# Degrees of an attention graph by way of DRAM, and its two layers on two head pairs at once

## The chip, the cores and the metric

One core of one Trainium2 chip runs the whole program. The metric is device time in microseconds (us); three runs of the kernel before gave 1188.17, 1189.1 and 1192.54 us.

## What is computed

The input has 16 batches of 256 tokens of 128 numbers. Each batch goes through an attention with 16 heads of 64 numbers, and its attention matrix also serves as a graph:

```
q, k, v = layer_norm(x) @ Wq, Wk, Wv          # 16 heads
attn = softmax(causal(q @ k.T))                # 256 x 256 per head
out  = attn @ v
adj  = clip(attn + eye, 0, 1);  deg = sum(adj, -1)
feats = v
for l in range(2):
    feats = gelu((adj @ (feats @ gnn_w[l] + gnn_b[l])) / deg + feats)
out  = layer_norm((out + feats @ lin_w + lin_b) @ Wo)
```

A mixture of 8 experts (two per token) follows; it runs as a separate stage after the 16 batches, and the change doesn't touch it, but for the loading of its weights.

The kernel does not compute attn @ v. It computes M = (adj / deg) @ v, subtracts v, and multiplies by deg: attn @ v = deg * (M - v). deg is thus wanted in a layout with the head's 64 numbers along the partitions and the 256 tokens along the free axis, the same deg in all 64 partitions of a head.

## The kernel before, in words

Heads go in 8 pairs, a pair being 128 partitions wide. Every engine has an order written out by hand in a function `batch(b, before, routed, after)`, which runs batch b and, woven in, the end of batch b-1, the routing of b-2 and the start of b+1. It is unrolled for batches 0, 1 and 15; a loop runs 2 to 14. Engines meet only through semaphores; each executes in order, so a wait holds up all that stands behind it.

The steps of pair n that matter here:

- `queries_keys`, `scores` on TensorE, `maxima` on VectorE (L1396), `exps` on ScalarE (L1118), `adjacency` on VectorE (L1406 to L1411, which also gives `den` and 1/sum in `rs`), `weights` on VectorE (L1420), `graph` on GpSimd (L495, L497: divides by the degree), `transposes` on TensorE (L743 to L746) and `graph` on ScalarE (copies into `gt0`, `gt1`).
- Degrees: GpSimd's `degrees` (L506) writes den * rs 64 times side by side into `deg`, 128x256; TensorE's `degrees` (L769) turns it with two transposes into the upper half of PSUM bank 5.
- Mixed values: TensorE's `differences` puts M into the lower half of bank 5 (8 matmul instructions); VectorE's `difference` (L1425) subtracts v into `dT`, `attended` (L1430) multiplies by the degrees in bank 5 into `aT`; ScalarE's `mixed_values` copies M into `gvT`.
- Layer 1: `layer1` on TensorE, `layer1_out` on VectorE (L1445), `gelu1` on ScalarE (L1142). Layer 2: `layer2_in` on TensorE and its copy on ScalarE, `layer2` on TensorE (8 matmul instructions), `layer2_out` on VectorE (L1451), `gelu2` on ScalarE (L1156).
- `output_attended` and `output_graph` add the pair's share of the projection in bank 7.

An f32 product shows as two matmul instructions in the trace, so one `layer1` is 2, one `layer2_in` 4. L633 is the line of the helper that issues all products. `norm_step(after, i)` and `norm_tokens(before, i)` on VectorE are the layer norms of the next and the last batch; some wait for a power taken on GpSimd (L489, L513). The queue of SyncE (SP) loads the inputs, clears `slots` in DRAM (33 DMAs of 520 KB, L364), loads the experts' weights (L373, L377: the DMA of expert e waits until expert e-2's were split by VectorE, L1458, and GpSimd, L537), and is then idle until the experts' stage. In the first batch, VectorE waits (in `small_weights` and for `w_x`) until the rest of x has landed.

Of the kernel before, what the change touches and what calls it, by code (L numbers as in the profile page):

```python
# [19 lines left out]
P = 128  # L20
BATCHES, TOKENS, DIM = 16, 256, 128
HEADS, DHEAD = 16, 64
PAIRS = HEADS // 2
TILES = TOKENS // P
# [20 lines left out]
CLEAR = 8  # L45
# [27 lines left out]
def build_program(nc, x, wq, wk, wv, wvT, gnn_w, gnn_b, lin_wT, lin_b, wo, gamma_in, gamma_out,  # L73
                  norm_w, routerT, guT, downT, alpha, slots, pairs, out):
# [9 lines left out]
    with ctx:  # L84
# [39 lines left out]
        zero = sb("zero", [P, CLEAR * ROW])  # L124
# [35 lines left out]
        gu_lo = sb("gu_lo", [P, EXPERTS, 2 * HID], f32r)  # L160

# [18 lines left out]
        deg = at("deg", [P, 3, 4, DHEAD])  # L180
# [4 lines left out]
        gvT = at("gvT", [P, PAIRS, TOKENS])  # L185
        vT = at("vT", [P, PAIRS, TOKENS])
        aT = at("aT", [P, PAIRS, TOKENS])
        f1T = at("f1T", [P, 4, TOKENS])
        g1 = at("g1", [P, 2, TILES, P])
        dT = at("dT", [P, TOKENS])  # L190
        z1 = at("z1", [P, 2, TOKENS])
        z2 = at("z2", [P, 2, TOKENS])
        f2T = at("f2T", [P, 4, TOKENS])
# [63 lines left out]
        p_deg = Signal(sem("p_deg"), PAIRS)  # L257
# [3 lines left out]
        a_d = Signal(sem("a_d"), PAIRS)  # L261
        d_d = Signal(sem("d_d"), PAIRS)
        s_deg = Signal(sem("s_deg"), PAIRS)
        d_a = Signal(sem("d_a"), PAIRS)

        s_f1, d_z1 = Signal(sem("s_f1"), PAIRS), Signal(sem("d_z1"), PAIRS)
        a_f1 = Signal(sem("a_f1"), PAIRS)
        s_g1, a_g1 = Signal(sem("s_g1"), PAIRS), Signal(sem("a_g1"), PAIRS)
        s_h2, d_z2 = Signal(sem("s_h2"), PAIRS), Signal(sem("d_z2"), PAIRS)
        a_f2, s_og = Signal(sem("a_f2"), PAIRS), Signal(sem("s_og"), PAIRS)  # L270
# [46 lines left out]
        L1_BANK, L2_IN_BANK, L2_BANK = 0, 2, 1  # L317
        MIX, DEG = slice(0, TOKENS), slice(TOKENS, 2 * TOKENS)
# [17 lines left out]
        def _(sp):  # L336
# [24 lines left out]

            sp.wait_ge(k_consts, 1)
            for r in range(0, SLOT_ROWS, CLEAR * P):
                sp.dma_start(slots[r:r + CLEAR * P, :].rearrange("(p r) d -> p (r d)", p=P),  # L364
                             zero[:, :]).then_inc(w_clear, 16)

# [7 lines left out]
            for e in range(EXPERTS):  # L374
                if e >= 2:
                    sp.wait_ge(k_gu_lo, e - 1)
                sp.dma_start(raw_gu[:, e % 2, :], guT[e]).then_inc(w_gu[e % 2], 16)  # L377
# [54 lines left out]
        def _(pool):  # L432
# [68 lines left out]
            def degrees(b, n):  # L501

                s = n % 3
                if n >= 3:
                    s_deg.wait(pool, b, n - 2)
                nc.gpsimd.tensor_tensor(deg[:, s], den[:, s, :].unsqueeze(2).to_broadcast([P, 4, DHEAD]),  # L506
                                        rs[:, s, :].unsqueeze(2).to_broadcast([P, 4, DHEAD]),
                                        ALU.mult).then_inc(p_deg.sem, 1)

# [30 lines left out]
            def batch(b, before, routed, after):  # L540

                graph(b, 0)
                degrees(b, 0)
                graph(b, 1)
                degrees(b, 1)
                graph(b, 2)
                graph(b, 3)
                degrees(b, 2)
                degrees(b, 3)
                graph(b, 4)  # L550
                if after is not None:
                    deviation(after, 0, 3)
                if before is not None:
                    token_power(before, 0)
                degrees(b, 4)
                if routed is not None:
                    d_pl.wait(pool, routed, 5)
                graph(b, 5)
# [3 lines left out]
                degrees(b, 5)  # L562
                graph(b, 6)
                graph(b, 7)
                degrees(b, 6)
                if after is not None:
                    deviation(after, 1, 7)
                degrees(b, 7)
                if after is None:
                    for e in range(0, 3):  # L570
                        gate_up_low(e)
# [4 lines left out]
                if after is None:  # L576
                    for e in range(3, 6):
                        gate_up_low(e)
                if before is not None:
                    token_power(before, 2)  # L580
                if after is None:
                    for e in range(6, EXPERTS):
# [1463 lines left out]
```

## Time and profile before

| what | us |
|---|---|
| median of three runs | 1189.1 |
| the profiled execution, its own time | 1183.16 |
| its span, first to last instruction | 1181.3 |
| TensorE busy in the span | 1088.6 |
| VectorE busy | 913.0 |
| ScalarE busy | 806.1 |
| GpSimd busy | 497.6 |

The profile is of one execution. "PE" is TensorE, "DVE" VectorE, "ACT" ScalarE, "POOL" GpSimd. A duration in the timeline is from an instruction's start to its end; neighbours on one engine overlap, so what an instruction takes from its engine is the distance from its start to the next one's start, called its pitch below. The mean granted clock of TensorE is 0.982 of full speed.

### The profile page before, as it was taken

The numbers are of one execution on the slowest core, as the hardware profiler recorded it, in microseconds if no ns is written. First come the engines' busy times: TensorE is split into PE (matmuls) and PEld (weight loads), VectorE is DVE, ScalarE is ACT, GpSimd is POOL, SyncE is SP. The second block draws the span as 40 slices with busy tenths as digits, with TensorE's granted clock in tenths as the row PEclk, the third lists the DMA queues.
The fourth block names the chain that finished last, engine by engine and source line by source line (L and its number), as shares of the span: only waits on it lengthen the run. The fifth ranks groups of instructions, "written<-read, shape, count | busy, mean of one in ns | idle before, by whom it ended". The sixth has DMA issues, their size and how long they took to land.

```text
span 1181.3 us, 28227 instructions
## 1 busy us (share of the span) xinstructions
PE 1088.6 (92%) x8320; PEld 863.9 (73%) x8320; DVE 913.0 (77%) x3755; ACT 806.1 (68%) x2351; POOL 497.6 (42%) x648
## 2 busy tenths in 40 slices
PE   5999999999999999999999999999999977898993
PEld 4677777777777777777777777777777756888993
DVE  5658797979797979797979797979788895566556
ACT  4678686768686868686868686868686853565662
POOL 4324253525353534343434344444444362545444
PEclk9899999999999999999999999999999998999997
DMA  6960000000000000000000000000000011222227
GB/s 201 405 231 1 2 3 9 5 6 3 8 3 8 1 10 1 10 1 10 1 10 1 10 1 10 1 10 1 10 1 9 2 55 49 60 55 63 62 62 221
DMA packets 37311, 47.41 MB, mean 40 GB/s; under 512 B 6009, under 2 KB 28539, under 8 KB 37200
## 3 DMA queue, kind: packets, MB, share of 16 engines
q1 hardware_dynamic: 32880, 37.81, 10.2%
q0 software_dynamic: 4320, 8.47, 2.1%
q14 instruction: 84, 0.69, 0.2%
q8 instruction: 27, 0.44, 0.2%
HBM read 18.14 MB, written 28.58 MB: 40 GB/s over the span
## 4 chain that ended last, share of the span: by engine, by line
PE 57%; DVE 29%; issue 8%; DMA 3%; SPq 1%; POOL 1%; ACT 1%; DVEq 0%; POOLq 0%
PE bank L633 46%; DVE eb L1411 5%; DVE nmax L1396 5%; DVE ea L1408 3%; PE bank L730 3%; DVE dT L1425 2%; PE bank L1000 2%; PE bank L769 1%; PE bank L743 1%; DVE z L1445 1%; DVE ratio L1755 1%; PE bank L746 1%; PE bank L744 1%; DMA pairs<-zout,zin 1%; DVE t L1656 1%
## 5 line engine op out<-in xcount | busy, mean ns | idle before, releaser
L495 POOL TENSOR_TENSOR ea<-ea,wgt 128x256 f32<-128x256 f32 x128 | 78.3, 612 | 400.1 <-DVE wgt L1420 400.1
L1396 DVE TENSOR_REDUCE nmax<-bank 128x1 f32<-128x128 f32 (+1 forms) x512 | 152.0, 346 | 60.5 <-PE bank L633 48.4
L1086 ACT ACTIVATE gt<-bank 128x512 f32<-128x512 f32 (+1 forms) x256 | 111.5, 491 | 66.6 <-PE bank L746 66.5
L1118 ACT ACTIVATE ea<-bank,nmax 128x128 f32<-128x128 f32 x256 | 96.0, 375 | 62.3 <-DVE nmax L1396 56.5
L633 PE MATMUL bank<-gt,g 128*64 128x256 f32 (+1 forms) x1024 | 112.8, 341 | 24.3 <-DVE z L1451 24.3
L497 POOL TENSOR_TENSOR eb<-eb,wgt 128x512 f32<-128x512 f32 x128 | 132.9, 1039 | 0.0
L1118 ACT ACTIVATE eb<-bank,nmax 128x256 f32<-128x256 f32 x256 | 123.3, 482 | 0.0
L633 PE MATMUL bank<-gt,vnat 128*64 128x256 f32 (+1 forms) x1024 | 111.5, 337 | 12.0 <-ACT gvT L1086 11.0
L633 PE MATMUL bank<-qk 64*128 64x128 f32 (+1 forms) x1024 | 119.3, 351 | 0.0
L1411 DVE SCALAR_TENSOR_TENSOR eb<-idw,ssum,eb 128x256 f32<-128x256 f32 x256 | 118.4, 500 | 0.0
L633 PEld LDWEIGHTS bank<-gt,g 128*64 128x64 f32 x1024 | 65.9, 137 | 61.1 <-issue 33.6
L523 POOL DMA_INDIRECT pairs<-zout,zin x71 | 69.7, 982 | 95.9 <-DVE zout L1942 89.6
L633 PEld LDWEIGHTS bank<-gt,vnat 128*64 128x64 f32 x1024 | 67.5, 136 | 58.2 <-issue 33.6
L1156 ACT ACTIVATE f2T<-z,gb 128x256 f32<-128x256 f32 x128 | 63.8, 515 | 62.3 <-DVE z L1451 62.3
L513 POOL TENSOR_TENSOR rs<-ve,half 128x2 f32<-128x2 f32 x48 | 33.3, 693 | 146.1 <-DVE ve L1701 96.1
L1451 DVE TENSOR_TENSOR z<-bank,f1T 128x256 f32<-128x256 f32 x128 | 54.1, 423 | 50.0 <-PE bank L633 48.9
L633 PEld LDWEIGHTS bank<-qk 64*128 64x128 f32 x1024 | 67.5, 187 | 27.1 <-issue 27.1
L1935 DVE TENSOR_TENSOR shid<-bank,ssg 128x352 f32<-128x352 f32 x71 | 37.2, 525 | 59.9 <-ACT ssg L1267 45.2
L1408 DVE SCALAR_TENSOR_TENSOR ea<-ident,ssum,ea 128x128 f32<-128x128 f32 x256 | 83.0, 362 | 0.0
L633 PE MATMUL bank<-gvT,gw 128*128 128x256 f32 x256 | 80.7, 397 | 1.2 <-DVE z L1445 0.2
L633 PE MATMUL bank<-xt_lo,w_hi 128*128 128x256 f32 x256 | 79.7, 311 | 2.2 <-DVE xt_lo L1389 2.2
L1086 ACT ACTIVATE qk<-bank 128x512 f32<-128x512 f32 x128 | 78.1, 610 | 5.1 <-PE bank L633 5.1
(231 smaller groups left out, 3207.9 us busy)
## 6 DMA issues: line engine op xcount, KB each, us to landing
slots<-zero SPq DMA_DIRECT2D x33, 520.0 KB, 15.2
zin<-slots SPq DMA_DIRECT2D x71, 65.0 KB
got<-pairs SPq DMA_DIRECT2D x8, 512.0 KB, 6.9
raw_gu<-in_guT SPq DMA_DIRECT2D x8, 352.0 KB, 2.9
out<-x_all SPq DMA_DIRECT2D x8, 256.0 KB, 2.6
pairs<-zout,zin POOLq DMA_INDIRECT x71
dn<-in_downT SPq DMA_DIRECT2D x2, 512.0 KB, 16.6
slots<-z,row_now POOLq DMA_INDIRECT x64, 2.3
```

The costliest lines, as they stand in the source:

```text
L495: nc.gpsimd.tensor_tensor(ea[:, s], ea[:, s], wgt[:, s, 0:2].unsqueeze(2).to_broadcast([P, 2, P]), ALU.mult)
L497: nc.gpsimd.tensor_tensor(eb[:, s], eb[:, s], wgt[:, s, 2:4].unsqueeze(2).to_broadcast([P, 2, 2 * P]), ALU.mult).then_inc(p_g.sem, 1)
L523: nc.gpsimd.indirect_dma_start(pairs, bass.IndirectOffsetOnAxis(ap=zin[:, j % RING, ID:ID + 1].bitcast(u32), axis=0), zout[:, j % RING, :] ...
L633: return nc_mm(o, st, mo, start=first, stop=last, **more)
L1086: return nc.scalar.activation(o, i, ACT.Copy, **more)
L1118: done = nc.scalar.activation(e[:, s, a, :], score_bank(n, a)[:, TILE_SCORES[t]], ACT.Exp, bias=nmax[:, s, i:i + 1], accum_out=ssum[:, s, ...
L1156: nc.scalar.activation(f2T[:, n % 4, :], z2[:, n % 2, :], ACT.Gelu, bias=gb[:, 1:2]).then_inc(a_f2.sem, 1)
L1396: done = V.tensor_reduce(nmax[:, n % 3, i:i + 1], score_bank(n, a)[:, TILE_SCORES[t]], X, ALU.max, negate=True)
L1408: V.scalar_tensor_tensor(ea[:, s, a, :], ident[:, :], ssum[:, s, a:a + 1], ea[:, s, a, :], ALU.mult, ALU.max, accum_out=den[:, s, a:a + 1])
L1411: done = V.scalar_tensor_tensor(eb[:, s, a, :], idw[:, :], ssum[:, s, 2 + a:3 + a], eb[:, s, a, :], ALU.mult, ALU.max, accum_out=den[:, s, ...
L1451: V.tensor_tensor(z2[:, n % 2, :], bank[L2_BANK][:, 0:TOKENS], f1T[:, n % 4, :], ALU.add).then_inc(d_z2.sem, 1)
L1935: V.tensor_tensor(shid[:, j % 2, 0:HID], bank[2 + j % 2][:, 0:HID], ssg[:, j % 2, :], ALU.mult).then_inc(d_hid.sem, 1)
```

## The change

Pairs 2d and 2d+1 form a double d (four in a batch, DOUBLES = 4). `differences`, `difference`, `attended`, `mixed_values`, `layer1`, `layer1_out`, `gelu1`, `layer2_in`, `layer2`, `layer2_out` and `gelu2` run once per double on 512 columns, each with one wait and one signal. The number of matmul instructions of a double is twice that of a pair.

GpSimd's and TensorE's `degrees` are gone. VectorE multiplies den * rs for a double (two instructions on 4 numbers per partition) into `dg`; SP writes these 1024 numbers, each by itself, to DRAM in the order of the tokens, waits until they have landed, and reads each row of 512 back into 64 partitions of `dgb`. VectorE's `attended` waits for that and takes both operands from SBUF.

```diff
+            def degrees(b, d):                       # sync
+                k = b * DOUBLES + d
+                d_dg.wait(sp, b, d + 1)
+                sp.dma_start(degs[2 * k:2 * k + 2, :].rearrange("a (j p) -> p (a j)", p=P),
+                             dg[:, d].rearrange("p a m t -> p (a m t)"),
+                             allow_slow_non_contiguous=True).then_inc(w_dg, 16)
+                sp.wait_ge(w_dg, 16 * (k + 1))
+                if k >= 2:
+                    sp.wait_ge(d_a.sem, k - 1)
+                for a in range(2):
+                    sp.dma_start(dgb[a * DHEAD:(a + 1) * DHEAD, d % 2, :],
+                                 degs[2 * k + a:2 * k + a + 1, :].to_broadcast([DHEAD, 2 * TOKENS])).then_inc(w_dgb.sem, 16)
...
+            pieces, ahead = SLOT_ROWS // (CLEAR * P), 9
             sp.wait_ge(k_consts, 1)
+            clear(0, ahead)
+            for k in range(2 * DOUBLES):
+                degrees(k // DOUBLES, k % DOUBLES)
+                clear(ahead + k * (pieces - ahead) // (2 * DOUBLES), ahead + (k + 1) * (pieces - ahead) // (2 * DOUBLES))
...
+            for e in range(2):
+                sp.dma_start(raw_gu[:, e % 2, :], guT[e]).then_inc(w_gu[e % 2], 16)
+            for b in range(2, BATCHES):
+                for d in range(DOUBLES):
+                    degrees(b, d)
+            for e in range(2, EXPERTS):
+                sp.wait_ge(k_gu_lo, e - 1)
...
+            def differences(b, d):                   # tensor
+                a_gt.wait(pe, b, 2 * d + 2)
+                if d >= 1:
+                    a_d.wait(pe, b, d)
+                for m in range(2):
+                    n = 2 * d + m
+                    mm = mixed(bank[5][:, m * TOKENS:(m + 1) * TOKENS],
+                               lambda t, a: vnat[:, t, n * P + a * DHEAD:n * P + (a + 1) * DHEAD], n)
+                mm.then_inc(s_mix.sem, 1)
...
-            def attended(b, n):                      # vector
-                d_d.wait(dve, b, n + 1)
-                V.tensor_tensor(aT[:, n, :], bank[5][:, DEG], dT[:, :], ALU.mult).then_inc(d_a.sem, 1)
+            def degrees(b, d):
+                d_e.wait(dve, b, 2 * d + 2)
+                for m in range(2):
+                    s = (2 * d + m) % 3
+                    done = V.tensor_tensor(dg[:, d, :, m, :].rearrange("p a t -> p t a"),
+                                           den[:, s, :].rearrange("p (t a) -> p t a", t=TILES),
+                                           rs[:, s, :].rearrange("p (t a) -> p t a", t=TILES), ALU.mult)
+                done.then_inc(d_dg.sem, 1)
+            def attended(b, d):
+                d_d.wait(dve, b, d + 1)
+                w_dgb.wait(dve, b, 32 * (d + 1))
+                V.tensor_tensor(aT[:, 2 * d:2 * d + 2, :], dgb[:, d % 2, :].rearrange("p (n i) -> p n i", n=2),
+                                dT[:, :].rearrange("p (n i) -> p n i", n=2), ALU.mult).then_inc(d_a.sem, 1)
```

All four orders in `batch` are written anew for the doubles. Those that the steps of the prediction speak of: in VectorE's,

```diff
                 maxima(b, 0, 1)
+                if before is None:
+                    small_weights()
+                    dve.wait_ge(w_x, 16)
...
+                maxima(b, 1, 0)
+                adjacency(b, 0)
...
-                maxima(b, 1, 1)
-                if before is None:
-                    small_weights()
-                    dve.wait_ge(w_x, 16)
...
+                weights(b, 2)
+                degrees(b, 0)
+                maxima(b, 4, 0)
+                maxima(b, 4, 1)
+                norm_step(after, 3)
+                adjacency(b, 3)
+                adjacency(b, 4)
+                weights(b, 3)
+                output_bias(before)
+                weights(b, 4)
+                norm_step(after, 4)
+                maxima(b, 5, 0)
+                maxima(b, 5, 1)
+                degrees(b, 1)
+                difference(b, 0)
+                output_kept(before)
+                adjacency(b, 5)
+                maxima(b, 6, 0)
+                weights(b, 5)
+                attended(b, 0)
...
+                layer1_out(b, 2)
+                norm_tokens(before, 6)
+                norm_tokens(before, 7)
+                degrees(b, 3)
+                norm_tokens(before, 8)
+                attended(b, 2)
+                x_low(after)
+                difference(b, 3)
```

and in TensorE's, for the end of a batch,

```diff
+                output_attended(b, 0)
+                layer1(b, 0)
+                output_attended(b, 1)
+                differences(b, 2)
+                layer1(b, 1)
+                transposes(b, 6)
+                layer2_in(b, 0)
+                layer1(b, 2)
+                layer2(b, 0)
...
+                layer2_in(b, 1)
+                output_attended(b, 2)
+                transposes(b, 7)
+                layer2(b, 1)
+                differences(b, 3)
+                layer2_in(b, 2)
+                output_graph(b, 0)
+                output_graph(b, 1)
+                layer1(b, 3)
+                layer2(b, 2)
+                output_graph(b, 2)
+                layer2_in(b, 3)
+                queries_keys(after, 0, b)
+                tokens_transposed(before, bank[6], after)
+                layer2(b, 3)
+                output_graph(b, 3)
+                queries_keys(after, 1)
+                values(after, 0, b)
```

Three of the last batch's `output_attended` more (3 to 7 instead of 5 to 7) run after it. `zero`, the source of the clears, now lies in the memory of `gu_lo`, and `gvT`, `f1T` and `f2T` hold two doubles each.

## Rows read from the trace of the kernel before

**Rows 1.** Busy by stretch, one turn, last batch: us, PE, PEld, DVE, ACT, POOL; clock, DMA.

```profile
617.50:677.10 59.60, 57.09 (x447) 43.76 (x446) 49.81 (x217) 43.81 (x135) 24.93 (x33) 1.00 0.02 5
...
915.50:975.00 59.50, 51.44 (x392) 39.47 (x390) 53.58 (x200) 39.47 (x123) 30.90 (x35) 0.97 0.10 30
```

**Rows 2.** Chain that ended last, one turn: start, us, what.

```profile
657.73 0.42 DVE z L1451
...
692.49 0.92 DVE ratio L1755
...
717.33 0.42 DVE z L1451
```

**Rows 3.** Timeline, TensorE: start, us, line, count.

```profile
607.37 0.87 PE L633 MATMUL bank<-gt,g 128*64 128x256 f32 x8
608.17 0.44 PE L769 MATMUL bank<-ident,deg 128*128 128x128 f32 x2
608.44 0.60 PE L633 MATMUL bank<-gvT,gw 128*128 128x256 f32 x2
608.88 0.61 PE L633 MATMUL bank<-gw,f1T 128*128 128x128 f32 x4
609.32 1.46 PE L633 MATMUL bank<-f2T,lwo 128*128 128x256 f32 x6
610.62 0.59 PE L633 MATMUL bank<-gvT,gw 128*128 128x256 f32 x2
```

**Rows 4.** Timeline, VectorE: start, us, line, count.

```profile
641.72 0.17 DVE L1406 RECIPROCAL rs<-ssum 128x4 f32<-128x4 f32 x1
...
643.14 0.42 DVE L1425 TENSOR_TENSOR dT<-bank,vT 128x256 f32<-128x256 f32 x1
643.47 0.17 DVE L1420 RECIPROCAL wgt<-den 128x4 f32<-128x4 f32 x1
643.60 0.42 DVE L1430 TENSOR_TENSOR aT<-bank,dT 128x256 f32<-128x256 f32 x1
...
648.89 1.14 DVE L1396 TENSOR_REDUCE nmax<-bank 128x1 f32<-128x128 f32 x4
649.95 0.41 DVE L1445 TENSOR_TENSOR z<-bank,vT 128x256 f32<-128x256 f32 x1
```

**Rows 5.** Groups of the loop by form: busy, mean ns of one.

```profile
L1396 DVE TENSOR_REDUCE nmax<-bank 128x1 f32<-128x256 f32 x176 | 72.8, 413 | 0.0
...
L1396 DVE TENSOR_REDUCE nmax<-bank 128x1 f32<-128x128 f32 x176 | 49.0, 278 | 35.1 <-PE bank L633 23.2 <-issue 11.1
```

**Rows 6.** Timeline, VectorE: three waits inside an instruction.

```profile
632.87 0.91 DVE L1755 TENSOR_SCALAR ratio<-ratio 128x2 f32<-128x2 f32 x1
...
638.82 0.52 DVE L1773 TENSOR_TENSOR place<-pre_sb,next_row 128x32 f32<-128x32 f32 x1
...
655.62 2.19 DVE L1656 TENSOR_SCALAR t<-y_now,mv,rs 128x128 f32<-128x128 f32 x2
```

**Rows 7.** Timeline, GpSimd, at the same times.

```profile
632.72 1.04 POOL L497 TENSOR_TENSOR eb<-eb,wgt 128x512 f32<-128x512 f32 x1
...
638.26 1.04 POOL L497 TENSOR_TENSOR eb<-eb,wgt 128x512 f32<-128x512 f32 x1
...
656.69 1.03 POOL L497 TENSOR_TENSOR eb<-eb,wgt 128x512 f32<-128x512 f32 x1
```

**Rows 8.** DMAs: size and median from issue to landing.

```profile
got<-pairs SPq DMA_DIRECT2D x8, 512.0 KB, 6.9
raw_gu<-in_guT SPq DMA_DIRECT2D x8, 352.0 KB, 2.9
...
gout<-in_gamma_out SPq DMA_DIRECT2D x1, 64.0 KB, 2.5
...
normw<-in_norm_w SPq DMA_DIRECT2D x1, 0.5 KB, 2.1
```

**Rows 9.** Waits in the first batch: us, times, longest.

```profile
DVE stat L1349 <- DMA x_all<-in_x: 4.8, 1, 4.8
```

More of the change, by code:

```diff
@@ L561, in batch @@
                         scatter(routed, c)
-                degrees(b, 5)
-                graph(b, 6)
                 graph(b, 7)
[L565 to L568, printed above, removed]
                 if after is None:
-                    for e in range(0, 3):
+                    for e in range(0, 2):
                         gate_up_low(e)
@@ L791, in layer2_in @@
[L791 to L805 removed]
+                    d_z1.wait(pe, b, d)
@@ new lines, in layer1, with layer2_in @@
+                for m in range(2):
+                    mm = product(bank[L1_BANK][:, m * TOKENS:(m + 1) * TOKENS], gw[:, 0, :], gvT[:, 2 * (d % 2) + m, :],
+                                 True, True)
+                mm.then_inc(s_f1.sem, 1)
+            def layer2_in(b, d):
+                a_f1.wait(pe, b, d + 1)
+                if L2_IN_BANKS[d] in (3, 4):
+                    a_gt.wait(pe, b, PAIRS)
+                if d >= 1:
+                    a_g1.wait(pe, b, d)
+                for i in range(2 * TILES):
+                    mm = product(bank[L2_IN_BANKS[d]][:, xt(i)], f1T[:, d % 2, xt(i)], gw[:, 1, :], True, True)
+                mm.then_inc(s_g1.sem, 1)
@@ L807, in output_start, with layer2 @@
+            def layer2(b, d):
+                a_g1.wait(pe, b, d + 1)
+                if L2_BANKS[d] in (3, 4):
+                    a_gt.wait(pe, b, PAIRS)
+                if d >= 1:
+                    d_z2.wait(pe, b, d)
+                for m in range(2):
+                    mm = mixed(bank[L2_BANKS[d]][:, m * TOKENS:(m + 1) * TOKENS],
+                               lambda t, a: g1[:, d % 2, m, t, a * DHEAD:(a + 1) * DHEAD], 2 * d + m)
+                mm.then_inc(s_h2.sem, 1)
             def output_start(b, before, routed):
@@ L937, in batch @@
-                if before is not None:
-                    tokens_transposed(before, bank[6], after)
-                if after is not None:
                     values(after, 0, b)
@@ L1182, in batch @@
                     folded_lin(0)
+                exps(b, 2, 1)
+                exps(b, 3, 0)
+                graph(b, 0)
                 exps(b, 3, 1)
-                graph(b, 1)
-                mixed_values(b, 0)
                 queries_keys(b, 5)
@@ L1201, in batch @@
                 graph(b, 4)
-                mixed_values(b, 3)
+                mixed_values(b, 1)
+                graph(b, 5)
                 exps(b, 7, 0)
@@ L1466, in batch @@
                 maxima(b, 0, 1)
-                if routed is not None:
-                    choose(routed, 1)
-                maxima(b, 1, 0)
-                adjacency(b, 0)
-                weights(b, 0)
-                maxima(b, 1, 1)
                 if before is None:
@@ L1477, in batch @@
                     norm_step(after, 0)
+                if routed is not None:
+                    choose(routed, 1)
+                maxima(b, 1, 0)
+                adjacency(b, 0)
+                if after is not None:
+                    norm_step(after, 1)
+                weights(b, 0)
+                maxima(b, 1, 1)
                 maxima(b, 2, 0)
@@ L1541, in batch @@
                     gate_up_high(0)
-                if after is not None:
-                    norm_step(after, 3)
-                layer1_out(b, 3)
+                    gate_up_high(1)
                 if after is None:
                     table_first(0)
-                weights(b, 7)
-                difference(b, 5)
-                if after is not None:
-                    norm_step(after, 4)
-                layer1_out(b, 4)
+                layer1_out(b, 2)
+                if before is not None:
+                    norm_tokens(before, 6)
+                    norm_tokens(before, 7)
```

532 lines of the change are left out of this document (211 added, 321 removed).

## The prediction

> **What bounds the kernel now.** I read the busy table by stretches first. One turn of the loop is 59.6 us, and in it TensorE is busy 57.09, VectorE 49.81, ScalarE 43.81 and GpSimd 24.93 [rows 1]. TensorE is idle for 2.5 us only. Then the chain of waits. It ends a stretch on VectorE with the `z` of 657.73, runs through TensorE alone until about 692, its products in a row without a gap, and from 692.49 to 717.33 through VectorE again, which is full there with maxima, adjacency and the small layer-norm steps; the pattern repeats after 717.33 - 657.73 = 59.60 us [rows 2]. So the turn has two limits that take turns: TensorE for 34 us, VectorE for 26 us, and in VectorE's part TensorE is nearly full too. A change that takes work off TensorE pays in the first part at once, and in the second only if VectorE gets shorter or TensorE's work moves there. What counts is the pitch, the distance between starts.
>
> **TensorE, removed.** The two transposes of a pair's degrees have a pitch of 608.44 - 608.17 = 0.27 us [rows 3]; where nothing waits it should be the 0.44 / 4 x 2 = 0.22 of two 128-column instructions of layer 2's input [rows 3]. I take 0.24. Eight of them are 1.9 us a turn. The number of all other products stays. What the doubles save is the hand-over between groups: a mixed product has a pitch of 0.80 [rows 3], while its four 256-column and four 128-column instructions, two side by side, would take 2 x 0.217 + 2 x 0.11 = 0.65 (0.217 is 1.30 / 6 from the output products, 0.11 as above [rows 3]). But layer 1's product and its neighbour have 0.44 each [rows 3], which leaves nothing to save. 16 groups go (32 become 16): between 0 and 16 x 0.15 = 2.4 us, and I take 0.05 each, 0.8 us, because most groups look like the tight ones. TensorE: -2.7 us a turn.
>
> **VectorE.** The four kinds of operation that become double took a pitch of 0.33 on 256 columns [rows 4]. Going from 128 to 256 columns adds 413 - 278 = 135 ns [rows 5], so 256 more add 0.27, and a double takes 0.60. Each kind goes from 8 x 0.33 = 2.64 to 4 x 0.60 = 2.40; four kinds save 1.0 us. The eight small products den * rs are new, at the 0.13 of a small operation in the queue (643.60 - 643.47, the pitch of `weights` [rows 4]): 1.0 us. VectorE comes out even, so its 26 us don't shrink by its own work.
>
> **ScalarE and GpSimd.** ScalarE's fixed cost is paid 16 times less; it is not on the chain, so this is worth nothing beyond the slack it gives. GpSimd loses eight `degrees`, some 5 of its 24.93 us, and is on the chain only through holds of VectorE (below).
>
> **What of it lies on the path.** Walking through the new orders with these pitches, TensorE's own work is some 54 to 55 us a turn. I find three places where it waits. `layer1` of double 1 wants bank 0 back from `layer1_out` of double 0, which stands in VectorE's order behind the placing of tokens: about 1.3 us. `layer1` of double 2 wants the same and `mixed_values`: about 1 us. And `transposes` of pair 7 wants GpSimd, which has the four scatters in front of its last `graph`: some 0.6 us. That is 2.9 us against the 2.5 us idle of now, the same within what such a walk can tell. I therefore take the turn to be shorter by TensorE's saving: -2.7 us.
>
> **The new wait.** `attended` now waits for two DMAs in series: the write of 1024 single numbers, and the read of rows into 64 partitions. No row shows such a write. A DMA of 128 single numbers lands in 2.1 us [rows 8]; if more pieces cost nothing this is the lower end. The upper end is by the 512 pieces of 1 KB of `got`, 6.9 us: (6.9 - 2.1) / 384 = 12.5 ns a piece makes 13.3 us for 1024. Those move 512 KB each and run several at a time, ours 4 KB and alone, so I take 4.2 us, nearer to the low end. The read is like the load of `gout`, one row spread over partitions, 2.5 us [rows 8]. With 0.8 for SP's two hand-overs and the second read's issue (an estimate), the chain takes 7.5 us, with ends 5.1 and 16.6.
>
> The Trainium skill's page "DMA: Bandwidth & Descriptors" says in its rules for kernel authors that a non-contiguous last dimension becomes one descriptor per element, and in its specifications that pieces below 512 B are read, modified and written. It names no time for a 4-byte write, and speaks for the upper half of the range.
>
> How much stands between `degrees` and `attended` on VectorE? For double 0: five maxima at 0.53 (1.06 / 2 [rows 4]), three `adjacency` at 1.42 (643.14 - 641.72 [rows 4]), three `weights`, the small `norm_step` and output steps (some 1.7 in all), two small products and one `difference`: about 9.8 us. Double 1 has about 11, double 2 about 9, by the same count. Double 3 has only 5.5 of work, but in TensorE's part VectorE also waits, and nothing needs it before the next batch's scores, some 4 us later. So 7.5 us is covered everywhere, 9 us just so. Behind a late `attended` stand `maxima`, and so `exps` and all the rest of the batch.
>
> **Once only.** In the first batch VectorE's wait for the rest of x (4.8 us [rows 9]) moves ahead of two maxima, one `adjacency` and one `weights`: 2 x 0.53 + 1.42 + 0.13 = 2.6 us of work is now done after it, which eats that batch's 2.7. In the last batch the load of expert 2's weights stands on SP behind the last degrees: 4.2 + 0.3 for the write, some 0.8 of issues, 2.9 for the load [rows 8], less about 2.7 of VectorE's work in between, gives a stall of 5.5 us before its split; against -2.7 that is +3. The clears, spread over two batches instead of one, are needed by batch 2 only; nothing waits for them, and a degree's write finds at most three of them in front of it and mostly none. Moving `zero` and the smaller buffers costs nothing: a buffer of two doubles holds the same four pairs as before, and `gvT`'s smaller room is behind a product that is long done.
>
> **Sum.** Fourteen turns (batches 1 to 14) at -2.7 are -38; the first batch 0, the last +3: -35 us. From the profiled execution's 1183.16 us that is 1148 us; its time lies 5.9 below the median of 1189.1, so against the median it is 1154.
>
> **Rival 1, the degrees come late (slower).** The place is `attended` of doubles 0 and 2; a stall at 0 gives double 1 its room, one at 2 gives it to 3. With a chain of L us a turn pays (L - 9.8) + (L - 9). At 10.75 this is 2.7 and the gain is gone; at 12 it is 5.2, so +2.5 a turn, +35 in all, 1224 us; at the upper end of 16.6 it is over 1340. For it: 1024 separate writes, and nothing in the profile that has the like. Against it: every small DMA here lands in 2.1 to 2.9 us.
>
> **Rival 2, GpSimd holds VectorE.** A `ratio` step on two numbers took 0.91 us, from 632.87 to 633.78, while GpSimd worked from 632.72 to 633.76; two layer-norm steps together took 2.19 us until 657.81, GpSimd until 657.72; a product of 32 columns with both operands in SBUF took 0.52 [rows 6, 7]. `attended` read its degrees from PSUM until now and reads both operands from SBUF in the new kernel; the eight small products do too. Twelve such instructions, GpSimd busy for a third of the turn (20 of 59.6), half a GpSimd operation of 1.04 each time: 12 x 1/3 x 0.5 = 2 us, of which some 1.3 would fall where VectorE is the limit. The turn then gains 1.4 and the time is 1189.1 - 20 + 3 = 1172. Against it: GpSimd has 5 us less to do, so that the old holds (1.65 us in the layer-norm steps alone) become rarer. The Trainium skill's "GPSIMD Engine Reference", key points, has the same rule: GpSimd shares its SBUF interfaces with VectorE, which contend for instructions in a two-port mode or with two SBUF inputs. By that rule, the rows agree.
>
> **Rival 3, coarser steps.** Each link of the layers' chain (product, add, gelu, product, copy, product) is longer by 0.27 and more, and only four doubles are there to overlap instead of eight pairs. If TensorE's waits in its own part grow by the 2.7 that it saves, nothing is won: 1189 to 1192. For it: the three waits found above are all of this kind. Against it: the new orders put other work (projection, next batch's queries) between the links.
>
> **How the numbers follow.** The forecast (the degrees covered, TensorE's saving comes through, with 2 to 4 us a turn) has 0.52; rival 2 has 0.18, rival 3 0.12, rival 1 0.18. The likeliest time is 1154. The low end takes the whole 2.4 of hand-overs and a fifth fewer holds: -4.3 a turn, -60, +3, so 1132; the high end takes in rivals 2 and 3 and the mildest of rival 1: 1200. A measurement of this kernel can tell about 0.5% (6 us) from no change. Faster: the forecast and rival 2 and a sliver of the third, 0.72. Same: 0.08. Slower: rival 1 and the rest of 3, 0.20.
>
> **What would show it.** In the changed kernel's trace: a turn of about 56.9 us; no line of degrees' transposes; TensorE's idle time in a turn still about 2.5; SP's write landing in about 4 us and the read in 2.5; no idle time of VectorE in front of `attended`. An `attended` of well over 0.6 us, ending with an operation of GpSimd, would be rival 2; idle time in front of it until a DMA, rival 1; TensorE idle until `z` or `gvT`, rival 3. A turn of 59 us or more makes the prediction wrong.

## The result and the profile after

The changed kernel takes 1400.9 us (median of four, 1394.4 to 1406.9), the kernel before 1188.6 beside it: a ratio of 1.178 [1.172, 1.184]. Times below are medians of the fast executions; one of e7's four, 1258.1 us, was over 1.5% above the fastest and is left out. The forecast was 1154 and its range ended at 1200, so it was wrong in sign and far outside. What came is Rival 1's mechanism, at more than Rival 1's price. The page of the profile after, its busy times, chain and costliest waiting group (the two profiled executions took 1406.93 and, before, 1183.16 us):

```profile
PE 1124.7 (80%) x8064; PEld 880.6 (63%) x8064; DVE 846.2 (60%) x3627; ACT 768.5 (55%) x2095; POOL 426.9 (30%) x520
...
DMA 40%; PE 29%; issue 13%; DVE 11%; SPq 5%; ACT 1%; POOL 0%; DVEq 0%; POOLq 0%
...
L1425 DVE TENSOR_TENSOR aT<-dgb,dT 128x512 f32<-128x512 f32 x64 | 45.1, 704 | 253.8 <-DMA dgb<-degs 253.7
```

A 40% share of DMA in the chain says that engines stand still for transfers, and the last line says where: 253.7 us in front of `attended`. Its own 704 ns are what it takes without any transfer too (708 in a turn of e1, below), so it isn't Rival 2. The turn from 720.09, measured between two copies of `pre_sb`, is 71.94 us instead of 59.60 [rows 1], with no more work in it but a lower clock:

```profile
720.09:792.03 71.94, 57.62 (x430) 43.25 (x430) 45.36 (x211) 41.74 (x119) 20.46 (x25) 0.93 0.11 19
```

SyncE's timeline (start and duration are of the issues) and VectorE's degrees and `attended` in the same time:

```profile
704.74 0.36 SPq L370 DMA_DIRECT2D degs<-dg  x1
715.03 1.08 SPq L377 DMA_DIRECT2D dgb<-degs  x2
716.16 0.59 SPq L370 DMA_DIRECT2D degs<-dg  x1
725.43 1.08 SPq L377 DMA_DIRECT2D dgb<-degs  x2
729.82 0.36 SPq L370 DMA_DIRECT2D degs<-dg  x1
739.64 1.35 SPq L377 DMA_DIRECT2D dgb<-degs  x2
741.03 0.59 SPq L370 DMA_DIRECT2D degs<-dg  x1
```

```profile
711.78 0.67 DVE L1407 TENSOR_TENSOR dg<-den,rs 128x4 f32<-128x4 f32 x2
718.54 0.69 DVE L1425 TENSOR_TENSOR aT<-dgb,dT 128x512 f32<-128x512 f32 x1 [3.13 <-DMA dgb<-degs]
728.95 0.69 DVE L1425 TENSOR_TENSOR aT<-dgb,dT 128x512 f32<-128x512 f32 x1 [3.63 <-DMA dgb<-degs]
729.56 0.23 DVE L1407 TENSOR_TENSOR dg<-den,rs 128x4 f32<-128x4 f32 x2
748.03 0.69 DVE L1425 TENSOR_TENSOR aT<-dgb,dT 128x512 f32<-128x512 f32 x1 [8.52 <-DMA dgb<-degs]
```

Three things can be read off. From the issue of the write to that of the read, which waits for it, 715.03 - 704.74 = 10.3 us pass, then 9.3 and 9.8: not the 4.2 of the forecast. The degrees of double 1 are ready at about 712, but SP takes them at 716.16 only, because until then it stood at double 0's write. And the read issued at 739.64, with the slow write of double 3 right behind it, lands at 748.0, after 8 us. The write itself is not moving data all that time (stretches of the changed kernel; the last two columns are the DMA engines' share and GB/s):

```profile
705.00:706.00 1.00, 1.00 (x9) 0.95 (x8) 1.00 (x6) 0.77 (x4) 1.00 (x2) 1.00 0.25 2
706.00:707.00 1.00, 1.00 (x7) 0.91 (x6) 1.00 (x7) 1.00 (x7) 0.28 (x1) 1.00 0.21 2
707.00:708.00 1.00, 1.00 (x6) 0.62 (x4) 1.00 (x8) 1.00 (x4) 0.00 (x0) 1.00 0.00 0
```

Its pieces pass from 705 to 707, and the share is 0.00 from there to 715, until its landing is signalled. The Trainium skill's page "DMA: Bandwidth & Descriptors", in "Anatomy of one DMA", puts most of a transfer's fixed time, which it gives as about 2.0 us and constant, on the receipt of the write from memory, HBM being the heaviest. It speaks there of transfers issued by GpSimd; this one is SP's. The eight silent microseconds agree with the place, and not with the figure.

Cut into parts by the first and the last of the 14 copies of `pre_sb` up to the last batch's and by the first load of the experts' stage, in us:

| | first batch until | a turn, mean of 13 | last part |
|---|---|---|---|
| before | 162.0 | 59.58 | 46.7 |
| changed | 221.6 | 71.24 | 60.2 |
| without the transfers (e1) | 162.2 | 56.12 | 43.6 |
| slow writes that nobody waits for (e7) | 180.0 | 60.88 | 62.3 |

### The profile page after: what moved, and what is told of

Its sections match the earlier page's. It is cut to its first block, busy times and chain, and to the rows that moved or that the text cites. A ratio compares the mean times of both kernels' runs of the same rounds, so it can differ in the third digit from the quotient of the medians.

```text
span 1405.1 us, 27144 instructions
## 1 busy us (share of the span) xinstructions
PE 1124.7 (80%) x8064; PEld 880.6 (63%) x8064; DVE 846.2 (60%) x3627; ACT 768.5 (55%) x2095; POOL 426.9 (30%) x520
## 4 chain that ended last, share of the span: by engine, by line
DMA 40%; PE 29%; issue 13%; DVE 11%; SPq 5%; ACT 1%; POOL 0%; DVEq 0%; POOLq 0%
DMA degs<-dg 29%; PE bank L639 25%; DMA dgb<-degs 10%; SPq L377 3%; DVE nmax L1376 2%; DVE eb L1392 2%; PE bank L992 2%; DVE ea L1389 1%; DMA x_all<-in_x 1%; PE bank L974 1%; DMA raw_gu<-in_guT 1%; PE bank L740 1%; SPq L364 1%; DVE x_all L1967 0%; DVE dg L1407 0%
## 5 line engine op out<-in xcount | busy, mean ns | idle before, releaser
L1425 DVE TENSOR_TENSOR aT<-dgb,dT 128x512 f32<-128x512 f32 x64 | 45.1, 704 | 253.8 <-DMA dgb<-degs 253.7
L639 PE MATMUL bank<-gvT,gw 128*128 128x256 f32 x256 | 89.5, 483 | 110.7 <-ACT gvT L1080 73.9
L639 PEld LDWEIGHTS bank<-gvT,gw 128*128 128x128 f32 x256 | 56.9, 239 | 129.4 <-ACT gvT L1080 114.5
L1080 ACT ACTIVATE gvT<-bank 128x512 f32<-128x512 f32 x64 | 38.5, 602 | 166.4 <-DVE dT L1417 151.2
L639 PE MATMUL bank<-gt,g 128*64 128x256 f32 (+1 forms) x1024 | 118.3, 382 | 8.8 <-ACT g L1080 8.4
L639 PE MATMUL bank<-gt,vnat 128*64 128x256 f32 (+1 forms) x1024 | 100.6, 340 | 15.4 <-ACT gt L1080 14.6
L639 PEld LDWEIGHTS bank<-gt,g 128*64 128x64 f32 x1024 | 74.5, 159 | 56.8 <-issue 28.8
L639 PE MATMUL bank<-xt_lo,w_hi 128*128 128x256 f32 x256 | 89.1, 348 | 1.6 <-DVE xt_lo L1369 1.6
L639 PE MATMUL bank<-gw,f1T 128*128 128x128 f32 x512 | 74.4, 291 | 19.3 <-ACT f1T L1139 18.2
L1153 ACT ACTIVATE f2T<-z,gb 128x512 f32<-128x512 f32 x64 | 46.2, 722 | 74.1 <-DVE z L1449 74.1
```

Source lines behind the costliest of these rows:

```text
L639: return nc_mm(o, st, mo, start=first, stop=last, **more)
L1080: return nc.scalar.activation(o, i, ACT.Copy, **more)
L1153: nc.scalar.activation(f2T[:, d % 2, :], z2[:, d % 2, :], ACT.Gelu, bias=gb[:, 1:2]).then_inc(a_f2.sem, 1)
L1425: V.tensor_tensor(aT[:, 2 * d:2 * d + 2, :], dgb[:, d % 2, :].rearrange("p (n i) -> p n i", n=2), dT[:, :].rearrange("p (n i) -> p n i", n ...
```

## The experiments

Theory A: it is the length of the chain write, read, `attended`, and what makes the write long is that its pieces are neighbours in memory. Theory B: making 1024 pieces costs it. Later a third stood beside them: the slow writes also hold up transfers with which they have nothing to do.

**m1, what a small transfer costs.** The kernel before, with 40 small DMAs on SP in a time when its queue is free, each waited for before the next.

```diff
+                for r in range(4):
+                    probe(tr_a[2 * r:2 * r + 2, :].rearrange("a (j p) -> p (a j)", p=P), pr[:, 0:8], ...)
...
+                    probe(tr_d[r, :, 0:1].rearrange("(j p) o -> p (j o)", p=P), pr[:, 0:8], ...)
```

> The kernel before, with 40 small DMAs on SP after the loads of the weights of experts 0 and 1, each waited for before the next is issued; nothing reads what they move. Theory A (the memory's confirmation of many 4-byte writes to DRAM is what takes the time; their packets moved in 2 us and then nothing moved for 8 us): 1024 numbers of 4 bytes to DRAM in the changed kernel's order land in 9 to 10 us; 128 pieces of 32 bytes in 2 to 2.5 us; 256 pieces of 16 bytes in 2.5 to 4 us; 256 single numbers in about 4 us; 1024 numbers with 64 bytes between them also in about 9 us if the count matters, in 3 to 4 us if neighbours in one line of memory hold each other up; 1024 single numbers read from DRAM in 3 to 4 us. Theory B (making the descriptors takes the time, whichever side they are on): the gather of 1024 single numbers from DRAM takes 9 to 10 us as well, and so do the spaced ones. Both: a row of 512 numbers spread over 64 partitions lands in 2.5 to 3 us; the kernel's own time stays at 1189 us.

SyncE's timeline of m1, a row for each kind, with its count:

```profile
75.91 31.39 SPq L370 DMA_DIRECT2D tr_a<-gu_lo  x4
115.26 5.45 SPq L370 DMA_DIRECT2D tr_b<-gu_lo  x4
121.80 23.62 SPq L370 DMA_DIRECT2D tr_c<-gu_lo  x4
153.33 9.33 SPq L370 DMA_DIRECT2D tr_d<-gu_lo  x4
165.07 6.31 SPq L370 DMA_DIRECT2D tr_a<-gu_lo  x4
173.57 13.93 SPq L370 DMA_DIRECT2D gu_lo<-gu_lo  x8
188.90 20.48 SPq L370 DMA_DIRECT2D gu_lo<-tr_a  x8
211.70 7.29 SPq L370 DMA_DIRECT2D gu_lo<-tr_b  x4
```

One takes the distance to the next row by the count. 1024 numbers side by side, as in the changed kernel: (115.26 - 75.91) / 4 = 9.8 us. 128 pieces of 32 B: 1.6. 256 single numbers side by side: 7.9. 1024 single numbers 64 B apart: (165.07 - 153.33) / 4 = 2.9. 256 pieces of 16 B: 2.1. The read of one row into 64 partitions: (211.70 - 188.90) / 8 = 2.85. The last row is 1024 single numbers read from DRAM; from its first issue to its fourth it is (7.29 - 0.36) / 3 = 2.3 us each, where Theory B had 9 to 10. So Theory B falls: a quarter of the pieces saves a fifth of the time, the same number of them further apart saves 70%, and as many in the other direction are quick. Theory A's "about 4 us" for 256 single numbers was wrong too: they took 7.9.

**e1, no transfers.** The changed kernel without the two DMAs and the wait; `attended` multiplies by a tile of ones, so the degrees are left out of the result.

```diff
-                sp.dma_start(degs[2 * k:2 * k + 2, :]...
...
-                w_dgb.wait(dve, b, 32 * (d + 1))
```

> The changed kernel without its DMAs of degrees: SP issues none, the wait in front of the last multiplication is gone, and that multiplication takes a constant tile instead of the degrees (the attention part of the output is left without them). Theory of the late chain: all of the 212 us lost, and more, come back; the turn is what the first forecast had, 56.9 us, and the time about 1154 us. Rival (the coarser steps or holds of VectorE by GpSimd cost something too): the turn stays above 59.6 us and the time above 1189 us.

1131.2 us (1130.1 to 1132.1), ratio 0.956 [0.954, 0.958]. The busy table of its turn:

```profile
555.39:611.54 56.15, 54.47 (x432) 41.63 (x431) 46.43 (x211) 41.73 (x119) 21.25 (x26) 1.00 0.01 5
```

All of the loss, and more, comes with the transfers. Everything else in the change is worth -4.4%, by TensorE's 57.09 [rows 1] - 54.47 = 2.62 us a turn and 0.8 less idle time of it.

**e2 and e3, larger pieces.** The same numbers as 256 pieces of 16 B, or as 512 of 8 B; `attended` puts them in order as it reads, in steps of 16 B or 8 B.

```diff
-                sp.dma_start(degs[2 * k:2 * k + 2, :].rearrange("a (j p) -> p (a j)", p=P),
+                sp.dma_start(degs[2 * k:2 * k + 2, :].rearrange("a (p c) -> p a c", p=P),          # e2
+                sp.dma_start(degs[2 * k:2 * k + 2, :].rearrange("a (m p t) -> p (a m) t", p=P, m=2),   # e3
```

> The changed kernel with the degrees written as 256 pieces of 16 bytes instead of 1024 of 4, in the order partition, pair, tile; the last multiplication reads them back with a stride of 16 bytes. Everything else is the same. Theory A: the write lands in 2.5 to 4 us instead of 9.3, the chain takes 6 to 8 us instead of 14, VectorE waits for it little or not at all, and the time is 1150 to 1200 us. Theory B gives a write of 9.3 / 4 + 2 = 4 us and the same time, so the probes must tell the two apart. If the chain's place in VectorE's order mattered more than its length, the time would stay above 1300 us. The stride makes the multiplication (0.69 us) no slower.

> As the version with 16-byte pieces, but with 512 pieces of 8 bytes, read back with a stride of 8 bytes. Theory C: the write lands in about 5 us, the chain takes 9 us, which the order of VectorE (7 to 11 us of room at the four doubles) covers but for double 3. The last multiplication, 1.09 us with a stride of 16 bytes against 0.69 without, takes 0.69 to 0.9. Time 1135 to 1150 us if the chain is covered, up to 1180 if not.

e2: 1141.7 us, ratio 0.965 [0.963, 0.967]; SP stood 106.1 us at its 64 writes, 1.7 each, and VectorE never in front of `attended`. But `attended` took 1.09 us instead of 0.69, by the step of 16 B; "no slower" was wrong. e3: 1139.5 us, 0.962 [0.959, 0.964]; 3.6 us at each write, 21.5 us in all in front of `attended`, whose 706 ns show that the step of 8 B costs nothing. A turn is 56.0 us. SyncE and VectorE of e3:

```profile
622.99 0.37 SPq L370 DMA_DIRECT2D degs<-dg  x1
626.27 1.08 SPq L376 DMA_DIRECT2D dgb<-degs  x2
631.46 0.36 SPq L370 DMA_DIRECT2D degs<-dg  x1
635.83 1.08 SPq L376 DMA_DIRECT2D dgb<-degs  x2
```

```profile
631.68 0.68 DVE L1424 TENSOR_TENSOR aT<-dgb,dT 128x512 f32<-128x512 f32 x1
639.29 0.69 DVE L1424 TENSOR_TENSOR aT<-dgb,dT 128x512 f32<-128x512 f32 x1 [0.79 <-DMA dgb<-degs]
```

A write of 3.3 to 4.4 us, the size that the forecast had assumed, is covered but for fractions. With it the change is what the forecast said, and better by 10 us (0.962 of 1189.1 is 1144).

**e6, the same single numbers, 64 B apart.** What m1 showed alone, in place; the read takes 512 numbers of the experts' weights instead, so the degrees are left out.

```diff
+                sp.dma_start(wide[k, :, 0:1].rearrange("(j p) o -> p (j o)", p=P),
```

> The changed kernel with each of the 1024 numbers put 64 bytes behind the last instead of 4 (m1: 2.9 us instead of 10.1). As many pieces, of the same 4 bytes, from the same places, and the same two reads with the same waits, but of 512 numbers of expert 0's weights, so the degrees are left out of the result. If it is the neighbourhood in memory that makes the write slow, and its length all that matters: a chain of 2.9 + 2.8 + 0.8 = 6.5 us, as in the two variants with larger pieces, so 1136 to 1150, and no waits for code. If the 1024 pieces themselves load the queue, 1200 or more.

1141.9 us (1139.9 to 1144.5), 0.961 [0.959, 0.963]. 64 writes of 1024 pieces of 4 B, as many as in the changed kernel, and 259 us less. So neither 1024 pieces nor 4 B a piece makes the loss by itself; what does is pieces of 4 B side by side.

**e4, a longer chain without a slow write.** e2 with two, or four, more writes of the same kind in front of each read.

```diff
+                for i in range(3):                    # e4_late4: range(5)
+                    sp.dma_start((degs if i == 0 else again)[...]).then_inc(w_dg, 16)
+                    sp.wait_ge(w_dg, 16 * (3 * k + i + 1))
```

> The version with 16-byte pieces, with two more writes of the same kind (2.1 us each, to memory that nobody reads) between the write and the read, each waited for: the chain goes from 6.0 to about 10.3 us. By the late chain, with room for 10.9, 10.0, 8.9 and 7.0 us at the four doubles as that version's trace has it, a turn pays some 1 to 3 us: 1155 to 1185 us.

> The same with four more writes: a chain of about 14.6 us, as long as in the changed kernel, but without any 4-byte write. If the length of the chain is all that matters: a turn pays (14.6 - 10.9) + (14.6 - 8.9) = 9.4 us and more where TensorE's clock falls in the idle time: 1290 to 1400 us. If the slow write also does harm in other ways (it holds up the read in front of it), this kernel stays well under 1400.

1242.2 us, 1.049 [1.045, 1.053], and 1503.4, 1.268 [1.263, 1.272]; both above what was expected, which went by the forecast's formula (doubles 0 and 2 pay, and 1 and 3 are served by them) with the rooms that e2's trace has, 10.9 and 8.9 us. From the one to the other a turn grew from 60.9 to 78.2 us. SyncE and VectorE of e4_late4:

```profile
603.51 0.37 SPq L371 DMA_DIRECT2D degs<-dg  x1
...
614.53 1.09 SPq L377 DMA_DIRECT2D dgb<-degs  x2
615.66 0.59 SPq L371 DMA_DIRECT2D degs<-dg  x1
...
625.81 1.09 SPq L377 DMA_DIRECT2D dgb<-degs  x2
630.60 0.37 SPq L371 DMA_DIRECT2D degs<-dg  x1
```

```profile
610.55 0.66 DVE L1407 TENSOR_TENSOR dg<-den,rs 128x4 f32<-128x4 f32 x2
618.00 1.06 DVE L1425 TENSOR_TENSOR aT<-dgb,dT 128x512 f32<-128x512 f32 x1 [3.82 <-DMA dgb<-degs]
629.29 1.09 DVE L1425 TENSOR_TENSOR aT<-dgb,dT 128x512 f32<-128x512 f32 x1 [3.04 <-DMA dgb<-degs]
630.28 0.29 DVE L1407 TENSOR_TENSOR dg<-den,rs 128x4 f32<-128x4 f32 x2
```

Double 1's degrees are ready at 611.2 and wait for SP until 615.66. `degrees` of double 2 stands in VectorE's order right behind `attended` of double 1. So from 603.28 to 630.28 the turn is two chains end to end: once a chain is longer than the distance of a double's degrees to the next (here some 7 us), the second chain starts late, whatever room it had of its own. Between 200 and 900 us SP stood 286.1 us at the writes of 47 doubles in e4_late2 and 344.8 at those of 36 in e4_late4, 6.1 and 9.6 each; with two more issues of 0.36 the chain grew by 4.2 us, and the turn by 17.3, about four times as much. The 4.2 us before these, from e2 (56.7) to e4_late2 (60.9), cost 4.2. Not all of the 17.3 is length: the granted clock of these 700 us is 0.98 in e4_late2 and 0.87 in e4_late4, and TensorE's busy time in a turn went from 55.6 to 62.7 us; how the 17.3 splits is not shown. No write of single numbers side by side is in these kernels, so a long chain, with the clock that falls in its waits, is enough for a loss as large as the changed kernel's.

**m2, two writes, and a read with a write behind it.** The kernel before with other small DMAs.

```diff
+                    sp.dma_start(pb[0:DHEAD, :], tr_b[0:1, 0:512].to_broadcast(...)).then_inc(w_probe, 16)
+                    sp.dma_start(pb[DHEAD:, :], tr_b[1:2, 0:512].to_broadcast(...)).then_inc(w_probe, 16)
+                    sp.dma_start(tr_a[0:2, :].rearrange("a (j p) -> p (a j)", p=P), pr[:, 0:8], ...)
```

> The kernel before with other probes on SP, four of each, in this order. Theory C (writes from several DMA engines to one line of memory hold each other up; the first probes had 10 us with 16 numbers in 64 bytes, 2.9 with one): 1024 numbers of 4 bytes, 8 bytes apart: about 6 us; 16 bytes apart: about 4; 32 bytes apart: about 3. 512 pieces of 8 bytes: about 5 us. 1024 single numbers side by side but in the order of the partitions, so that 8 neighbours come from one partition: under 4 us if writes of several partitions are what collides, about 10 us if the number of writes in a line counts, whoever makes them. Two slow writes at once to different rows: 10 to 11 us together if lines work in parallel, about 20 if the memory takes them one after another. A read of two rows into 64 partitions each with a slow write issued right behind: the read lands in 8 us, as it did once a turn in the changed kernel, against 3 to 3.5 alone.

```profile
172.44 65.18 SPq L385 DMA_DIRECT2D tr_a<-gu_lo  x8
254.98 0.50 SPq L390 DMA_DIRECT2D gu_lo<-tr_b  x1
255.53 0.60 SPq L391 DMA_DIRECT2D gu_lo<-tr_b  x1
256.17 0.59 SPq L392 DMA_DIRECT2D tr_a<-gu_lo  x1
264.12 0.34 SPq L396 DMA_DIRECT2D gu_lo<-tr_b  x1
```

Two slow writes issued together land after (254.98 - 172.44) / 4 = 20.6 us: one after the other. A pair of reads with such a write behind it takes 264.12 - 254.98 = 9.1 us (then 8.5, 6.1 and 5.1), where a single read alone has 2.85 and a pair with a quick write behind it 3.5 (614.53 to 618.00 in e4_late4). The read of 739.64 above fits this. That of 715.03, which also had a slow write right behind it, landed by 718.54, in 3.5 us: a read is not held every time. And something not looked for: the whole kernel took 1232.5 us beside 1183.8, though only the SP queue, free at that time, had been given work. Its trace has waits that it puts to "issue" or "remote" (no releaser is seen), of up to 10.9 us on VectorE, 8.7 on ScalarE and 10.5 on GpSimd, where the kernel before has 2.8 at most. The time is lost while the probes run: the turn from 162.57 took 102.0 us and the next 62.9, the later ones 59.6 as before. m1, with four slow writes of 1024 and four of 256, has no such wait on VectorE or ScalarE; so not every slow write does it.

**e7, slow writes beside the work.** e1 with the slow writes put back, and nothing waiting for their data but SP and, one turn later, `degrees`, which never had to stand for them; the degrees are left out of the result as in e1.

```diff
+                sp.dma_start(degs[2 * k:2 * k + 2, :].rearrange("a (j p) -> p (a j)", p=P), dg[:, d]...).then_inc(w_dg, 16)
+                sp.wait_ge(w_dg, 16 * (k + 1))
...
+                if b > 0:
+                    dve.wait_ge(w_dg, 16 * ((b - 1) * DOUBLES + d + 1))
```

> The kernel without the transfers (1131 us) plus the 64 writes of 1024 single numbers, with which SyncE alone is busy: no engine waits for them except VectorE, a whole turn later, before it writes the same degrees tile again, and nothing is read back (attended multiplies by a tile of ones, so the degrees are left out of the result). Theory A, the slow write hurts by the length of the chain alone, which is not here: at most 2 us over 1131, so 1130 to 1136. Theory B, a slow write also holds up other transfers that engines stand for, the loading of their own code among them (m2 showed waits of up to 10.9 us that the trace puts to issue or to an unknown releaser on VectorE, ScalarE and GpSimd, and 49 us in all for 36 slow writes; the changed kernel shows 53 us of these on ScalarE): 64 writes give 1160 to 1210, with such waits in the trace.

1238.7 us (1234.9 to 1247.3), 1.045 [1.040, 1.050]: 108 us over e1 (106 by the ratios, since it ran on another chip) for writes that nobody needs. A third of it has a plain cause, which the expectation left out: other transfers stand behind these writes on SP's queue. GpSimd stands for the clears before the first copy of `pre_sb`, VectorE for expert 2's weights in the last batch:

```profile
159.76 0.61 POOL L514 TENSOR_TENSOR ea<-ea,wgt 128x256 f32<-128x256 f32 x1 [33.00 <-DMA slots<-gu_lo]
1014.02 0.53 DVE L1453 CAST gu_hi<-raw_gu 128x704 fp32r<-128x704 f32 x1 [12.32 <-DMA raw_gu<-in_guT]
```

In these parts e7 loses 17.8 and 18.7 us against e1 (table above). What is left is 13 turns of 4.8 us, 62 us, in which no wait for SP's queue is seen. One of them, VectorE of e7 and its stretches:

```profile
309.16 0.59 DVE L1637 TENSOR_SCALAR t<-y_now,mv,rs 128x128 f32<-128x128 f32 x2
316.98 0.69 DVE L1415 TENSOR_TENSOR dT<-bank,vT 128x512 f32<-128x512 f32 x1 [7.23 <-remote]
```

```profile
310.00:312.00 2.00, 0.96 (x9) 0.77 (x7) 0.00 (x0) 0.00 (x0) 1.39 (x3) 1.00 0.10 33
312.00:314.00 2.00, 0.00 (x0) 0.00 (x0) 0.00 (x0) 0.00 (x0) 1.70 (x2) 0.84 0.48 69
...
316.00:318.00 2.00, 0.00 (x0) 0.00 (x0) 1.02 (x3) 0.30 (x1) 0.00 (x0) 0.50 0.05 0
318.00:320.00 2.00, 1.25 (x3) 1.10 (x4) 2.00 (x11) 2.00 (x5) 0.00 (x0) 0.50 0.00 0
```

VectorE stands for 7.23 us although TensorE had given what `dT` reads, and ScalarE and TensorE wait for VectorE in turn. Such waits sum to 70.5 us on VectorE and 61.8 on ScalarE in e7, to 13.5 and 53.3 in the changed kernel, and to 0.2 and none in e1. Up to the first load of the experts' stage they are 62.6 and 45.9 in e7, 5.0 and 35.9 in the changed kernel, and none in e2, e3, e4 and e6. The slow writes are all that sets e7 apart from e1, so it is shown that they hold up more than their own queue. But e6, run beside e7, has 7.9 and 17.0 in the experts' stage, where no such write is left; so they are not the only cause of waits of this kind. That it is the engines' own code which comes late is argued: the profile lists two queues of the kind "instruction" (0.65 MB together in the changed kernel), but no event of theirs. The Trainium skill's "Runtime: NRT & Kernel Launch", in "Instruction fetch mechanics", says that each engine fetches its code by a DMA queue of its own while it works, "mostly hidden"; no run here shows that fetch by itself.

**e8 and e9, the weights out of the degrees' way.** e3, with the weights of expert 2 and on requested by GpSimd as soon as it has read the slot.

```diff
+                if e + 2 < EXPERTS:
+                    pool.wait_ge(k_gu_lo, e + 1)
+                    nc.gpsimd.dma_start(raw_gu[:, e % 2, :], guT[e + 2]).then_inc(w_gp[e % 2], 16)
```

> The variant with pieces of 8 bytes (1139.5 us), and the weights of experts 2 and on requested by GpSimd, right after it has read the slot's old ones, instead of by SyncE behind the degrees of the last batch. Forecast's last step: the last batch shows about 5 us of waiting for them that the kernel without transfers does not; these go, so 1133 to 1137. If the wait in the last batch has another cause, 1138 to 1142.

1147.7 us (1145.0 to 1151.1), 0.965 [0.963, 0.968]: not the gain expected, while its trace had the last part shorter by 4.1 us. It ran on another chip than e3, so both ran again together.

> The variant with pieces of 8 bytes again, now on the chip of its rival and in the same rounds: it had 1139.5 us beside 1183.7 of the kernel before, a ratio of 0.962. 0.958 to 0.966 again.

> The variant in which GpSimd requests the weights of experts 2 and on, again, beside the other. Its first run was 1147.65 us beside 1189.32, a ratio of 0.965, and its trace had 44.8 us from the last batch's placing to the first load of the experts' stage instead of 48.9. If these 4 us are real and the rest of the difference was the chip's, it is 3 to 4 us faster than the other here; if requesting by GpSimd costs something elsewhere (the first batch began 3 us later), it is equal or slower.

e9_8B 1142.6 us, 0.966 [0.963, 0.969]; e9_pool 1134.9 us (1132.7 to 1136.2), 0.958 [0.957, 0.960]. SyncE's loads of the weights in the last batch and the first load of the experts' stage, of e9_8B and then, without loads of weights on SyncE, of e9_pool:

```profile
926.04 17.34 SPq L399 DMA_DIRECT2D raw_gu<-in_guT  x6
949.98 4.33 SPq L425 DMA_DIRECT2D zin<-slots  x8
```

```profile
940.06 4.41 SPq L423 DMA_DIRECT2D zin<-slots  x8
```

From the last batch's `pre_sb` (900.49 and 895.22) it is 49.5 and 44.8 us: the stall is there, 4.6 us of the 7.7 between the medians. The other 3 I can't place; in these two traces the first batch ends at 172.1 and 166.8 us. e9_pool is the best version of this study, 50 us under the kernel before.

## Why the prediction was wrong

**What bounds the kernel; TensorE.** Right. The forecast took 2.7 us a turn off TensorE; e1 shows 2.62. It took the turn to be 56.9; without the transfers it is 56.1, in e2 56.7, in e3 56.0. The three waits of the walk (2.9 us) were too many: TensorE is idle for 56.15 - 54.47 = 1.7 us.

**VectorE.** Not even, as forecast, but shorter: 49.81 [rows 1] to 46.43. The operations of a double have the pitch that was worked out (720.18 to 720.79 in the changed kernel, 0.61). What was missed are old holds that went: the two layer-norm steps of 2.19 us [rows 6] take 0.67 in a turn of e1, and the 32 operations of `adjacency` 0.9 us less together (477 ns instead of 506, 332 instead of 358). That GpSimd's smaller load is the reason is argued. Rival 2's holds exist, the eight new products take 312 ns each, but they are outweighed.

**The new wait, the failing step.** "I take 4.2 us" for the write: it is 9.3 to 10.3. The lower end rested on a transfer of 128 single numbers from DRAM into SBUF [rows 8], the upper on pieces of 1 KB, and neither is a write to DRAM of neighbours of 4 B. The reason given for the low end ("4 KB and alone") was the error: the write's bytes take 2 us, and its end is silence. The read was right alone (2.85 for 2.5), and wrong once in the turn shown, with a slow write behind it (8). The true chain, 704.74 to 718.54, is 13.8 us, inside the ends of 5.1 and 16.6 that the text had and that its range did not keep (its own terms, 2.1 + 2.5 + 0.8, make the lower end 5.4).

**The rooms.** The second failing step. At 13.8 us Rival 1's formula gives (13.8 - 9.8) + (13.8 - 9) = 8.8 a turn; against e1 the turn lost 71.24 - 56.12 = 15.1. Missing were SP, which serves one double at a time, so that the chains stand end to end (e4), what the clock costs, and the harm that slow writes do beside the chain: 60.88 - 56.12 = 4.8 us of a turn (e7). How much of these 4.8 is in the changed kernel's 15.1 is not shown; its VectorE has far fewer of the waits without a releaser. By medians, 1131 becomes 1239 by the writes alone and 1401 by waiting for them.

**Once only.** For the kernel without the transfers, "the first batch 0" is right to 0.2 us. With them it was wrong: in the changed kernel the first batch's part ends 59 us later, and nine waits in front of `attended` make 54.6 us of it. e7's 18 us there are another thing: they come with GpSimd's wait for the clears, for which, by the forecast, "nothing waits"; in the changed kernel that holds, in e7 it doesn't. "Finds at most three of them in front of it" was no reason for nothing: with pieces of 8 B, writes right behind clears took 6.5 and 7.0 us (e3), those of a turn 3.1 to 4.4; in the changed kernel they took 10.7 to 13.1. The last batch's stall of 5.5 us for expert 2's weights was right in kind, and in size where the writes are quick: e2 has 48.7 us in the last part and e1 43.6, and e9_pool takes it away. In the changed kernel VectorE stood 12.3 us for these weights.

**The clock.** TensorE's mean granted clock fell from 0.982 to 0.903. In e7's rows it is 1.00 up to 312; TensorE does nothing in the next stretch (0.84), and from 316 to 320 it has 0.50, the level of 1.2 GHz, also where TensorE works again. So a wait costs more than its length; the forecast had no such term. Rival 3 isn't seen: TensorE's idle time in a turn of e1, 1.7 us, is shorter than before, not longer.

## What to carry to other kernels

A transfer whose like no row shows is to be priced by its worst neighbour, or measured alone before the kernel is built on it: direction, size of a piece and distance between pieces all mattered here, and the rows that gave the ends were both loads, not writes. Write small things to DRAM in pieces of 8 B or more, even if a reader has to reorder them; a step of 8 B cost VectorE nothing. When a queue serves several waits in order, count the chains end to end, and not each against its own room, and look at what else stands behind them on the queue.

## What the hardware showed that I had not expected

- Writes of 4 KB from SBUF to DRAM, alone, issue to issue: pieces of 4 B side by side 9.8 us (8.1 with a partition's eight in a row); 8, 16, 32, 64 B apart 5.1, 3.8, 2.9, 2.9; in pieces of 8 B 4.2; of 16 B 2.1; of 32 B 1.6. Only 256 numbers of 4 B side by side still 7.9.
- Such writes are served one after the other (20.6 us for two), they can delay a pair of reads issued before them (5.1 to 9.1 us in m2 instead of 3.5), and they hold up engines that wait for nothing on their queue (in e7, 62 us over 13 turns with 52 of them).
- A product of 512 columns with one SBUF operand in steps of 16 B takes 1.09 us, in steps of 8 B or 4 B 0.69.
